# A wide table of x and the degree factor in a graph network kernel: one set of gathers in place of two

## The reference, cut to what matters

```
h = relu(layernorm(x))                     # then a second layer norm inside the layer
deg  = segment_sum(edge_weight, src)
dinv = where(deg > 0, 1 / sqrt(deg), 0)    # the degree factor, one per node
w    = -(dinv[src] * edge_weight * dinv[dst])
prop(h) = segment_sum(w[:, None] * h[src], dst)
x = x + L0(h);  x = x + L1(relu(layernorm(x)));  ...
```

## Time and profile before

| | us |
|---|---|
| median of 3 runs | 7733.81 (7695.58 to 7745.73) |
| profiled execution, its own time | 7712.7 |
| its span, first to last instruction | 7710.9 |
| TensorE busy in the span | 4424.3 (57%) |
| VectorE | 4302.8 (56%) |
| ScalarE | 2412.5 (31%) |
| GpSimd | 4225.5 (55%) |
| mean granted TensorE clock | 0.691 of full speed |

### The profile page before, as it was taken

The page is one execution under the profiler, slowest core; times in us unless marked ns, Lnnn a source line. Parts: engine busy times, 40 slices in busy tenths (PEclk is TensorE's granted clock), DMA queues, the critical chain, the costliest instruction groups (busy, mean ns, idle before and its releaser), DMA issues. The chain is left out here.

```text
span 7710.9 us, 76126 instructions
## 1 busy us (share of the span) xinstructions
PE 4424.3 (57%) x15756; PEld 2083.4 (27%) x15804; DVE 4302.8 (56%) x6926; ACT 2412.5 (31%) x5349; POOL 4225.5 (55%) x3989
## 2 busy tenths in 40 slices
PE   7895555655555656577655638857863343554100
PEld 3332333333333333222211114423331111111000
DVE  6665555655565555344300079959983444777433
ACT  0002444444442222112122237723331113555211
POOL 7764444444444555566566514456646655664666
PEclk8997676767676777555566568878885556777555
DMA  1001222222222333111132223323323332222221
GB/s 25 7 0 42 89 88 94 88 94 88 93 88 76 79 73 78 46 49 52 50 76 75 70 75 113 113 55 80 80 77 87 97 98 65 62 59 55 61 62 53
DMA packets 444564, 541.94 MB, mean 70 GB/s; under 512 B 207490, under 2 KB 221960, under 8 KB 443641
## 3 DMA queue, kind: packets, MB, share of 16 engines
q1 hardware_dynamic: 319050, 449.36, 19.3%
q0 software_dynamic: 125440, 91.77, 6.6%
HBM read 302.04 MB, written 276.42 MB: 75 GB/s over the span
## 5 line engine op out<-in xcount | busy, mean ns | idle before, releaser
L1039 POOL DMA_INDIRECT l_got<-d_x,l_near x1176 | 1236.9, 1052 | 826.4 <-issue 375.1
L1039 POOL DMA_INDIRECT ln_xd<-in_x,ln_near x392 | 391.1, 998 | 851.1 <-issue 789.6
L722 PE MATMUL ps<-hot_lo,hot_w 128*128 128x512 bf16 x2304 | 547.8, 392 | 92.2 <-issue 73.3
L1039 POOL DMA_INDIRECT p_got<-d_ext,p_near x392 | 400.9, 1023 | 332.1 <-DMA p_near<-in_src_rows 204.7
L1039 POOL DMA_INDIRECT p_got<-d_tx,p_near x392 | 399.2, 1018 | 268.3 <-issue 227.7
L1039 POOL DMA_INDIRECT p_got<-d_h,p_near x392 | 397.0, 1013 | 251.3 <-issue 127.9
L608 POOL DMA_INDIRECT d_pos<-place,near x392 | 427.9, 1092 | 173.6 <-issue 116.2
L2240 POOL DMA_INDIRECT out<-fi_res,fi_near x392 | 381.5, 973 | 248.2 <-issue 171.1
L1198 DVE TENSOR_TENSOR_SCAN p_sums<-same,p_sums,ps 65x1024 f32<-65x1024 f32 (+3 forms) x98 | 229.4, 2340 | 476.7 <-remote 246.3
L1039 POOL DMA_INDIRECT ln_dd<-d_dinv,ln_near x392 | 391.1, 998 | 119.6 <-issue 119.6
L1672 POOL TENSOR_TENSOR at_own<-at_hd,at_al 128x1024 f32<-128x1024 f32 x49 | 195.5, 3990 | 403.0 <-ACT at_al L1766 357.1
(11 more groups left out here) (372 smaller groups left out, 11546.8 us busy)
## 6 DMA issues: line engine op xcount, KB each, us to landing
d_x<-ln_x SPq DMA_DIRECT2D x196, 256.0 KB, 2.1
l_xd<-d_x SPq DMA_DIRECT2D x147, 256.0 KB
d_ext<-ln_ext SPq DMA_DIRECT2D x98, 264.0 KB
ln_x<-in_x SPq DMA_DIRECT2D x98, 256.0 KB
d_h<-ln_hb SPq DMA_DIRECT2D x98, 256.0 KB, 2.1
d_x<-l_x SPq DMA_DIRECT2D x98, 256.0 KB
out<-d_x SPq DMA_DIRECT2D x49, 512.0 KB
l_got<-d_x,l_near POOLq DMA_INDIRECT x1176
```

What stands on the lines that cost most here:

```text
L722: last = nc.tensor.matmul(bank(h), hot_w[:, r, k], hot_lo[:, r, 512 * h:512 * h + 512], start=False, stop=False)
L1039: nc.gpsimd.indirect_dma_start(out=out[:, q], out_offset=None, in_=source, in_offset=bass.IndirectOffsetOnAxis(ap=ids[:, q:q + 1], axis=0) ...
```

## The change

A table `D.xt` of 65 columns, x and the degree factor, takes the place of two tables as the source of the gathers in the node run. Its first 64 columns come from a new input `x_wide` (x with a zero column, laid out before the launch), copied DRAM to DRAM in `degrees` by seven DMAs on ScalarE's queue. Its last column is written at the start of `lone_nodes`, by seven DMAs on ScalarE's queue from `D.dinv`. GpSimd waits for them, then gathers rows of 65 columns for all 49 edge groups by the ids in place, and stores each group itself after it has issued the next one's gathers. `near`, `dd`, `W.wdE` and VectorE's two operations on them go; SP's `store_xd` goes; the product with the edge weight is made in `first_propagation` from the 65th column. The tiles that hold `D.xd` rows get 65 columns.

```diff
+COLUMN_PARTS = 7
-        D.xd, D.tx1, D.hs = (dram("d_" + name, (EP, C)) for name in ("xd", "tx1", "hs"))
+        D.tx1, D.hs = (dram("d_" + name, (EP, C)) for name in ("tx1", "hs"))
+        D.xt, D.xd = dram("d_xt", (NP_, C + 1)), dram("d_xd", (EP, C + 1))
@@ degrees
+        blocks = lambda a: a.rearrange("(k q e) c -> k q (e c)", q=112, e=P)
             @block.scalar
             def _(act):
+                for k in range(NODE_GROUPS * S // 112):
+                    act.dma_start(blocks(D.xt)[k], blocks(A["x_wide"])[k]).then_inc(xt_in, 16)
                 act.wait_ge(pos_ready, 1)
...
                 nc.scalar.activation(root[:], deg[:], ACT.Sqrt).then_inc(rooted, 1)
+                act.wait_ge(xt_in, 16 * (NODE_GROUPS * S // 112))
@@ lone_nodes
-        near, xd, dd = t("near", [P, 2, S], I32), t("xd", [P, 2, S, C]), t("dd", [P, 2, S])
+        xd = t("xd", [P, RING, S, C + 1])
+        dstE = W.idsE[:, GROUPS:2 * GROUPS]
+        column = lambda a, k: a.rearrange("(k q n) c -> k q (n c)", k=COLUMN_PARTS, q=16)[k]
             @block.gpsimd
             def _(pool):
-                def gather(i, r, g):
-                    k, e = r // 2, half_turns(i, r)
-                    if r % 2 == 0:
-                        hold(pool, m["near_done"], e + 1)
-                        hold(pool, xd_st[k], i * 16 + 16)
-                        gather_rows(nc, pool, A["x"], near[:, k], xd[:, k], got_x[k], NP_ - 1)
-                    else:
-                        hold(pool, m["taken"], e - 1)
-                        gather_rows(nc, pool, D.dinv, near[:, k], dd[:, k].unsqueeze(2), got_d[k], NP_ - 1)
-                ring_loop(pool, NODE_GROUPS, [gather])
+                hold(pool, m["columns"], 16 * COLUMN_PARTS)
+                for e in range(GROUPS + 1):
+                    if e < GROUPS:
+                        hold(pool, xd_st[e % RING], 16 * (e // RING))
+                        gather_kept(nc, D.xt, dstE, e, xd[:, e % RING], got_x[e % RING], NP_ - 1)
+                    if e > 0:
+                        r = (e - 1) % RING
+                        hold(pool, got_x[r], 128 * ((e - 1) // RING) + 128)
+                        nc.gpsimd.dma_start(group_rows(D.xd)[e - 1], xd[:, r]).then_inc(xd_st[r], 16)
+                for r in range(RING):
+                    pool.wait_ge(xd_st[r], 16 * of_slot(r, GROUPS))
@@ sync
-                def store_xd(i, r, g):
-                    if r % 2 == 0:
-                        k, e = r // 2, half_turns(i, r)
-                        hold(sp, got_x[k], i * 128 + 128)
-                        sp.dma_start(group_rows(D.xd)[e], xd[:, k]).then_inc(xd_st[k], 16)
-                ring_loop(sp, NODE_GROUPS, [load], [store_xd], [store_ext], [], [store_h], [], [store])
+                ring_loop(sp, NODE_GROUPS, [load], [], [store_ext], [], [store_h], [], [store])
@@ vector: indices and take removed
-                ring_loop(dve, NODE_GROUPS, [a, indices], [], [h], [b, take], [scale_b], [c])
+                ring_loop(dve, NODE_GROUPS, [a], [], [h], [b], [scale_b], [c])
@@ scalar
+                for k in range(COLUMN_PARTS):
+                    act.dma_start(column(D.xt[:, C:C + 1], k), column(D.dinv, k), allow_slow_non_contiguous=True).then_inc(m["columns"], 16)
                 act.sem_inc(m["tabbed"], RING)
@@ first_propagation
-                    yield from norm.centre(nc, dve, g, xd[:, r])
+                    yield from norm.centre(nc, dve, g, xd[:, r, :, 0:C])
+                    yield 3
+                    nc.vector.scalar_tensor_tensor(out=wd[:, r % 2], in0=xd[:, r, :, C], scalar=-1.0, in1=of_group(W.ewE, g),
+                                                   op0=ALU.mult, op1=ALU.mult).then_inc(m["wd_done"], 1)
...
+                    dve.wait_ge(m["wd_done"], g + 1)
-                    nc.vector.tensor_tensor(w, got[:, r, :, C], of_group(W.wdE, g), ALU.mult).then_inc(m["weighed"], 1)
+                    nc.vector.tensor_tensor(w, got[:, r, :, C], wd[:, r % 2], ALU.mult).then_inc(m["weighed"], 1)
@@ attention_sums: xd tile with C + 1 columns, read as xd[:, r, :, 0:C]
@@ lay_out
+    a["x_wide"] = np.concatenate([a["x"], np.zeros((NP_, 1), x.dtype)], axis=1)
```

More of the change, by code:

```diff
@@ L560, in degrees @@
         landed = [sem(f"places_written{r}") for r in range(RING)]
+        xt_in = sem("wide_rows")
+        blocks = lambda a: a.rearrange("(k q e) c -> k q (e c)", q=112, e=P)
         loads = []
@@ L857, in _ @@
                     sp.sem_inc(h_st[r], 16)
-                for k in (0, 1):
-                    sp.sem_inc(xd_st[k], 16)
                 def load(i, r, g):
@@ L890, in _ @@
                     sp.wait_ge(h_st[r], 16 * (of_slot(r, NODE_GROUPS) + 1))
-                for k in (0, 1):
-                    sp.wait_ge(xd_st[k], ODD_EVEN[k] + 16)
             @block.vector
@@ L896, in _ @@
                 dve.sem_inc(m["x1_done"], RING)
-                def indices(i, r, g):
-                    if r % 2 == 0:
-                        k, e = r // 2, half_turns(i, r)
-                        after(dve, got_x[k], i * 128)
-                        after(dve, got_d[k], i * 128)
-                        nc.vector.tensor_scalar(near[:, k], of_group(W.idsE, e + GROUPS), 1, 0, ALU.mult, ALU.add
-                                                ).then_inc(m["near_done"], 1)
                 def h(i, r, g):
@@ L911, in h @@
                                                    op1=ALU.max).then_inc(m["h_done"], 1)
-                def take(i, r, g):
-                    if r % 2 == 1:
-                        k, e = r // 2, half_turns(i, r)
-                        dve.wait_ge(got_d[k], i * 128 + 128)
-                        nc.vector.scalar_tensor_tensor(out=of_group(W.wdE, e), in0=dd[:, k], scalar=-1.0,
-                                                       in1=of_group(W.ewE, e), op0=ALU.mult, op1=ALU.mult
-                                                       ).then_inc(m["taken"], 1)
                 def a(i, r, g):
@@ L1042, in gather_rows, with gather_kept @@
             bounds_check=limit, oob_is_err=False).then_inc(landed, 16)
+def gather_kept(nc, source, ids, g, out, landed, limit):
+    for q in range(S):
+        nc.gpsimd.indirect_dma_start(
+            out=out[:, q], out_offset=None, in_=source,
+            in_offset=bass.IndirectOffsetOnAxis(ap=ids[:, g, q:q + 1], axis=0),
+            bounds_check=limit, oob_is_err=False).then_inc(landed, 16)
 def first_propagation(nc, A, sem, W, D, bank):
@@ L1049, in first_propagation @@
         t = lambda n, sh, dt=F32: ctx.enter_context(nc.sbuf_tensor(n, sh, dt))
-        xd, g1 = (t("p1_" + n, [P, RING, S, C]) for n in ("xd", "g1"))
+        xd, g1 = t("p1_xd", [P, RING, S, C + 1]), t("p1_g1", [P, RING, S, C])
         got = t("p1_got", [P, RING, S, C + 2])
         near, ls, ls2 = (t("p1_" + n, [P, RING, S], I32) for n in ("near", "ls", "ls2"))
-        beyond = t("p1_beyond", [P, S])
+        beyond, wd = t("p1_beyond", [P, S]), t("p1_wd", [P, 2, S])
         msg, yd = t("p1_msg", [P, S, C + 1]), t("p1_yd", [P, S, C])
@@ L1626, in attention_sums @@
         hs, hd = (t("at_" + n, [P, 2, S, C]) for n in ("hs", "hd"))
-        xd, x1 = t("at_xd", [P, RING, S, C]), t("at_x1", [P, 2, S, C])
+        xd, x1 = t("at_xd", [P, RING, S, C + 1]), t("at_x1", [P, 2, S, C])
         alpha = t("at_alpha", [ALPHAS, 2, G_ROWS])
```

13 lines of the change are left out of this document (5 added, 8 removed).

## The result

The changed kernel takes 7,752.4 us in the median of 20 runs, the kernel before 7,727.6 in 20 runs beside them: ratio 1.0034, 95% interval 1.0018 to 1.0051. It is slower by a third of a per cent, 25 us, where the prediction had 57 us less.

The account below looks back on a forecast made before the run. It took long gather runs delaying other engines' semaphores to bound the node run. Terms -174 + 87 + 30 = -57 gave 7,656 us for the profiled execution, a median of 7,677, range 7,440 to 7,930.

Parts of the forecast that it names:

- (a): Node run: 392 factor gathers go, and the time lost to gather runs falls from 398 to 224 us: -174 us.
- (e): First stage: the copy of x on ScalarE's queue delays the first loads, bounds 0 to 56, middle taken: +30 us.
- (d): Node run's start: seven column DMAs keep ScalarE from its squares, 6 x 14.5 us: +87, bounds 3 to 102.
- dear-column rival: Node run: column elements cost four times 1.01 ns, ScalarE stands still 348 us: +204, 7,938 us; chance 0.10.
- the unbroken run: Node run: the remaining gathers and stores form one run of 574 us, losing 0.39 per us, 224 us.
- first rival: Node run: the unbroken run lets nothing catch up, 0.78 lost per us, 448 us: +167, 7,901 us; chance 0.27.
- base rhythm: Node run: an undisturbed step per node group takes 13.44 us, so 98 groups would take 1,317 us.
- loss share of 0.39: Node run: each us of gather run loses 0.39 us, from 398 us lost beside 1,021 us of runs.
- 13.9 us of the earlier trace: Node run: VectorE's addition starts 13.9 us after the matmuls it waits for end, read as a late semaphore.
- (b): Node run: SP's hold for the gather and its store go; already priced in the gathers' term, so 0.
- (c): VectorE loses 16 us of work in the node run, gains 8 in the next stage: 0, at most +8.
- predicted tell-tales: Gathers 770 to 1,340, steps 20 to 25 us, stage about 1,660, first square 80 to 100, VectorE 20 to 60.

Follow-up runs that it names:

- e6: The changed kernel, run again without edits: 7,699.6 us, 1.005 of the kernel before (7,652.6).
- e18: Changed kernel with the copy in 49 thin pieces, no column, gathers in one unbroken run: 7,510.8 us, 0.973 of the kernel before (7,715.3).
- e7: Changed kernel with gathers paced in runs of eight per two node groups, copy in 49 thin pieces by SP: 7,408.7 us, 0.967 of the kernel before.
- e8: e7 with each edge group's eight gathers cut into two runs of four, one per node group: 7,264.0 us, 0.940 of the kernel before (7,716.0).
- e5: The kernel before, unchanged, profiled again: 7,643.0 us, 0.999 of the kernel before in its set (7,652.6).
- run 1: No label of a run: the words belong to "node run 1,666", the time in us of the changed kernel's node run stage.
- e10: e7 with the column written by SP in 28 parts, the gathers following: 7,207.6 us, 0.935 of the kernel before (7,716.0).
- e14: Changed kernel with thin copy, column by SP in 28 parts, six gathers per node group in pairs: 6,197.0 us, 0.996 of the kernel before (6,220.9).
- e12: The kernel before with only the copy added, at the head of ScalarE's queue: 6,319.4 us, 1.017 of the kernel before (6,221.1).
- e15: The same kernel as e18, in the free condition: 6,197.2 us, 0.996 of the kernel before (6,220.9).
- e9: e7 with a wait ahead of each gather, giving runs of one and three: 7,157.5 us, 0.929 of the kernel before (7,716.0).
- e17: The same kernel as e14, in the held condition: 7,076.8 us, 0.918 of the kernel before (7,715.3).

## Why the prediction was wrong

The forecast was -57 us and the result +25: the wrong way. Part (a), the gathers, came out better than the forecast. What turned the sign is two terms that were too small, (e) first and (d) behind it. The mechanism beneath (a) was wrong as well, but its errors cancelled.

- **(e), the copy in front, +30.** This is the step that failed in the sum: it measured +99 and +141 where gathers hold back, +89 to +98 where they don't. With +99 in its place alone the forecast would have been +12. The start by itself is 59.5 us late, near the upper bound I had (56). By the Trainium skill, "DMA: Bandwidth & Descriptors", section Queues, rings and completion order, a DMA engine serves its queues in turn, a packet from each; that rule gave +56, and the trace agrees with it, with VectorE's first operation at 66.50 in place of 7.02. The pieces were other ones than I took: the trace has the copy as 448 pieces of 58,240 bytes, 2.7 us each, and three of the four loads go between them, 24 rows per engine, which makes 65 us. Time from issue to landing of these loads, before and after:

```profile
dnE<-in_next_part SPq DMA_DIRECT2D x1, 196.0 KB, 4.8
```

```profile
ewE<-in_ew_part SPq DMA_DIRECT2D x1, 196.0 KB, 25.5
idsE<-in_dst_part SPq DMA_DIRECT2D x1, 196.0 KB, 45.4
dnE<-in_next_part SPq DMA_DIRECT2D x1, 196.0 KB, 64.3
```

 I halved the bound without a row that asked for it. What no bound held was the second part: scatters that start late are made up in one long run, beside which TensorE falls back by some 38 us more (54 in e6). Of e6's 141 about 27 come later in the stage and lie within what the first stage varies by from one execution to another.
- **(d), the column, +87.** 119.5 us of ScalarE standing still, 131.9 in e6; the node run of the changed kernel is 128 longer than that of e18, e6's 148. 1.19 to 1.31 ns per element, not 1.01, and all seven pieces are waited for, not six. The dear-column rival, at four times the price, is out.
- **(a), the unbroken run, -174.** The node run of e18 alone measures it: 1,537.6 against 1,749.6 and 1,740.7, so -203 to -212 us (the whole of e18 is 0.973 of 7,715, -205). The size came out nearly right from two errors that cancel. The unbroken run loses 0.85 of its 551 us (470), not 0.39, and the kernel before lost up to 675, not 398. The mechanism was the first rival's, "lets nothing catch up"; it had 0.78, and 398 to set against it.
- **The base rhythm, 13.44 us.** This is the step of the mechanism that failed, and the loss share of 0.39 with it. I took the shorter of the two alternating steps of the earlier trace rows for an undisturbed one. It was not: a run of 16 holds the semaphores long enough that both steps of the pair pay. Undisturbed it is 10.61 us, 98 x 10.61 = 1,040, and 1,715 - 1,040 = 675 us were lost beside 1,021 us of runs, 0.66 of them. (Against the same kernel in the free condition it is 623 to 652, 0.61 to 0.64 of them: its own steps there are 10.80 to 11.03 us.) Nothing in the trace of before shows an undisturbed step, except at the stage's very end, where I didn't look for it: the steps of the last six groups are shorter, but there the pipeline is running empty.
- **The 13.9 us of the earlier trace rows.** I put them all down to one late semaphore. VectorE had other work before that addition and stood idle for 2.40 us only, as its bracket says. Its order was late already, because ScalarE had waited 9.13 us for transposes that ended at 1500.63:

```profile
1500.03 0.60 PE L970 MATMUL ps<-ident,ln_hf 128*128 128x128 f32 x4
...
1508.32 0.60 ACT L1023 ACTIVATE ln_hb<-ps 128x512 f32<-128x512 f32 x1 [9.13 <-remote]
```

 So semaphores come late in the middle of the run too, which began at 1493.28 and ended at 1513.83, and not only at its end.
- **(b), SP's hold, 0, and (c), VectorE's two operations and the 65th column, 0 to +8.** First propagation is 2.5 us longer. That SP's hold had no part of its own was not tested alone; e7 and e8, where SP waits for no gather, still lose by the length of the run.
- **The sum.** With the node runs and first stages of the profiled executions: -212 + 128 + 99 = +15 for the recorded pair, +18 with first propagation's 2.5; measured +25. For e5 and e6: -203 + 148 + 141 = +86; their profiled spans differ by 84, their medians by 57 (47 against the kernel before in the set). The predicted tell-tales read: gathers 911 to 1,462, not 770 to 1,340; steps of 35 to 111 us beside them (first rival) and 10.61 behind; first square 120 us into the stage; node run 1,666 where "about 1,660" was given, by luck, since a larger loss in the run (470 for 224) and a shorter undisturbed step (1,040 for 1,317 over the stage) nearly cancel; VectorE at 66.50, beyond the 20 to 60.

So the halving was worth what was hoped, and two moves that looked cheap, each placed where nothing covers it, gave it back. Placed differently the copy costs an estimated 2 to 12 us in the free condition (49 pieces; held, it is lost in what the first stage varies by), and the column about nothing (28 parts, e10 and e14).

## What to carry to other kernels

An alternating rhythm is no measure of the undisturbed one: look for a stretch without the disturber, or take it away in an experiment, before a loss is priced. Long runs of indirect DMAs on GpSimd can hold back all that the other engines tell each other: cut them into runs of three or fewer, with real pauses between, and tie them to events spread over a step of the main work. A bulk copy and a column of single elements cost what waits behind them, so cut them into pieces of a few us and put them beside work that runs ahead.

## What the runs showed of the hardware

- Two conditions of the same program: 6,217 to 6,221 us and 7,653 to 7,728 us for the kernel before. Only stages with indirect DMAs from GpSimd differ: attention_weights takes 111.7 us (e5) and 111.5 (e12), attention_sums 481.4 and 481.2 though GpSimd computes there too, but first propagation 695.2 and 556.6, the relu stage 657.3 and 535.9, the node run of the kernel before 1,740.7 and 1,097.7. What sets the condition, no run tells, and so the held-back semaphores are a finding of one condition: e15 and e18 are one kernel, with 1,067.8 and 1,537.6 us of node run.
- In the held condition the loss is nil for gathers in runs of one and three, 0.2 us per gather in runs of four, 0.8 (e7) or 0.5 (e10) in runs of eight, 1.2 in an unbroken run of 392. A gather's own length, 1.00 us, is the same throughout.
- In the free condition one unbroken run of 392 gathers costs the other engines nothing that shows: steps of 10.53 us beside it, 10.64 behind it (e15).
- A DRAM to DRAM write of single 4-byte elements takes 1.19 (the changed kernel's trace) to 1.32 ns each (e9), and ScalarE's queue holds the engine for that whole time when seven such DMAs of 14,336 follow each other; SP's, with 3,584 elements per step of 10.2 us, is held 0.5 us each, 1.3 at most (e10, e14, e17).
- A load of small rows on one hardware queue goes between the pieces of a copy on another: beside 58,240-byte pieces of 2.7 us, three loads of 128 rows of 1,568 bytes land 25.5, 45.4 and 64.3 us after their issue, where the last of them took 4.8 without the copy.
